# A fused window-mixer and routed-expert kernel: scatters in two groups and a normalisation in two halves

## The reference

```python
x = x + mixer(ln(x))                      # first half
t = x as tokens (16, 3136, 96)
t = t + experts(ln(t))                    # second half

def mixer(x):                             # windows of 7 x 7 positions
    w = ln(w, ln1_w, ln1_b)               # w: (1024 windows, 49 positions, 96)
    h[i] = w[i] @ Bm + h[i-1] @ A         # over the 49 positions
    xr = h @ Cm
    y = gelu(ln(xr, ln2_w, ln2_b) @ W1 + b1) @ W2 + b2    # 96 -> 384 -> 96
    return xr + y

def experts(t):                           # top 2 of 4 experts, exact gelu
    masked = softmax(t @ gate_w + gate_b) on the two best, renormalised
    return sum_e masked[e] * (gelu(t @ w1[e] + b1[e]) @ w2[e] + b2[e])
```

## Time and profile before

| | us |
|---|---|
| median of 3 runs | 1960.43 |
| lowest, highest | 1958.6, 1961.08 |
| the profiled execution | 1960.39 |
| its span | 1958.7 |
| PE busy in it | 1871.8 (96%) |
| ACT busy | 1599.1 (82%) |
| DVE busy | 1490.5 (76%) |
| POOL busy | 1355.4 (69%) |

### The profile page before, as it was taken

How to read it: one execution, slowest core, us unless ns; L and a number is a source line. 1 busy time by engine, 2 the same in 40 slices (tenths; PEclk the granted TensorE clock), 3 DMA queues, 4 the chain that set the end, 5 groups by cost and what they waited for, 6 DMA issues and landing times.

```text
span 1958.7 us, 36640 instructions
## 1 busy us (share of the span) xinstructions
PE 1871.8 (96%) x8883; PEld 1302.6 (67%) x8883; DVE 1490.5 (76%) x6676; ACT 1599.1 (82%) x3068; POOL 1355.4 (69%) x1097
## 2 busy tenths in 40 slices
PE   5979999999999999997599999999999999999996
PEld 3546666666666666664377777777777777777774
DVE  5767887788777877786477777777777777777775
ACT  3868887888888888875499989999999899999995
POOL 3357767776767677667477777777777777777775
PEclk9989999999999999998699999999999999999998
DMA  4042212222222222111666666666666666666662
GB/s 127 28 114 68 71 67 69 68 71 67 71 67 71 67 70 69 61 51 52 214 211 211 208 207 204 206 206 209 213 208 209 206 202 206 214 210 212 209 208 75
DMA packets 121158, 272.93 MB, mean 139 GB/s; under 512 B 26148, under 2 KB 34749, under 8 KB 120946
## 3 DMA queue, kind: packets, MB, share of 16 engines
q1 hardware_dynamic: 85840, 209.93, 35.6%
q0 software_dynamic: 32000, 58.87, 8.7%
q10 hardware_dynamic: 3106, 1.78, 0.3%
HBM read 204.47 MB, written 66.98 MB: 139 GB/s over the span
## 4 chain that ended last, share of the span: by engine, by line
PE 50%; POOL 27%; issue 20%; DVE 1%; DMA 1%; POOLq 0%; ACTq 0%; ACT 0%; SPq 0%; DVEq 0%
POOL sorted_rows L447 19%; PE mix_ps L1170 7%; PE mix_ps L1171 7%; PE mix_ps L1172 7%; POOL rstd_xt L436 7%; PE turn_ps L1156 4%; PE up_ps L1156 4%; PE turn_ps L1157 4%; PE turn_ps L1158 4%; PE up_ps L1157 4%; PE up_ps L1158 4%; PE tok_ps L1179 3%; PE y_ps L1142 2%; POOL rows L444 1%; POOL rstd_r L423 0%
## 5 line engine op out<-in xcount | busy, mean ns | idle before, releaser
L480 POOL DMA_INDIRECT out<-out_sb,idx x412 | 424.1, 1029 | 262.7 <-DVE out_sb L968 156.2
L924 DVE TENSOR_TENSOR g_lo<-g,g_hi 128x512 fp32r<-128x512 f32 x618 | 423.9, 686 | 198.5 <-ACT g_hi L613 198.5
L447 POOL DMA_INDIRECT sorted_rows<-rows,pos x392 | 383.3, 978 | 118.9 <-issue 104.8
L613 ACT CAST g_hi<-g 128x512 fp32r<-128x512 f32 x618 | 380.8, 616 | 13.1
L1048 PE MATMUL y_ps<-g,d_mlp 128*100 128x512 f32 x588 | 307.2, 604 | 6.5 <-ACT g L548 1.8
L469 POOL TENSOR_TENSOR ex<-euler,rows 128x16 f32<-128x16 f32 x103 | 305.2, 2963 | 10.1 <-DMA rows<-sorted_rows 9.7
L1170 PE MATMUL mix_ps<-g_hi,ew 128*96 128x512 f32 x618 | 244.1, 395 | 0.2 <-DVE g_lo L924 0.2
L1171 PE MATMUL mix_ps<-g_hi,ew 128*96 128x512 f32 x618 | 244.0, 395 | 0.0
L1172 PE MATMUL mix_ps<-g_lo,ew 128*96 128x512 f32 x618 | 243.7, 394 | 0.0
L548 ACT ACTIVATE g<-up_ps 128x512 f32<-128x512 f32 x294 | 172.7, 605 | 60.1 <-PE up_ps L1041 54.9
L423 POOL TENSOR_TENSOR rstd_r<-var_eps,neg_half 128x8 f32<-128x8 f32 x49 | 81.7, 1668 | 193.0 <-DVE var_eps L723 193.0
(11 more groups left out here) (181 smaller groups left out, 4164.9 us busy)
## 6 DMA issues: line engine op xcount, KB each, us to landing
ew<-expert_w SPq DMA_DIRECT2D x206, 384.0 KB, 4.2
ew<-expert_w SPq DMA_DIRECT2D x206, 288.5 KB, 3.5
rows<-sorted_rows SPq DMA_DIRECT2D x103, 394.0 KB
x_in<-in_x SPq DMA_DIRECT2D x49, 384.0 KB, 3.1
out<-out_sb,idx POOLq DMA_INDIRECT x412
sorted_rows<-rows,pos POOLq DMA_INDIRECT x392, 2.5
sorted_rows<-pad_rows SPq DMA_DIRECT2D x11, 394.0 KB, 5.0
expert_w<-w_hi SPq DMA_DIRECT2D x4, 192.0 KB, 3.9
```

The source lines that it names most:

```text
L447: pool.indirect_dma_start(out=sorted_rows[:, :], out_offset=bass.IndirectOffsetOnAxis(ap=pos[:, r, s:s + 1], axis=0), in_=rows[:, r, s, :] ...
L480: pool.indirect_dma_start(out=out_rows, out_offset=bass.IndirectOffsetOnAxis(ap=idx[:, r, s:s + 1], axis=0), in_=out_sb[:, r, s, :], in_of ...
L613: act.copy(g_hi[:, n % PART_RING, :], g[:, n % G_RING, :]).then_inc(hi_done, 1)
L924: dve.tensor_tensor(g_lo[:, n % PART_RING, :], g[:, n % G_RING, :], f(g_hi[:, n % PART_RING, :]), ALU.subtract).then_inc(lo_done, 1)
```

## The change

Three edits, all in phase 1.

- POOL: the eight scatters of a tile are issued as two groups of four. The first four (with the numbering) stay at the end of period t + 2. The last four stand at the start of period t + 3, ahead of `rstd_of_r`, behind a wait on `h_summed` for that period's input product. The loops get one more period for the last group.
- ACT: `normalise_xr` has two parts of four activations. Part 0 stands before Gelu 4 (it waits for the shift), part 1 behind Gelu 5 and the x_t copy. Part 0 signals a new semaphore `xr_half_ok`, part 1 `xr_n_ok`.
- PE: the xr transposes are issued as two groups of four, the first behind `xr_half_ok`, the second behind `xr_n_ok`. `turn_y(p,1)` moves from the end of period p to the next period, between `from_state` and `from_input`. The x transposes are issued by two calls without a wait between them.

```diff
--- before.py
+++ after.py
@@ -84,7 +84,7 @@
 
 
 def periods():
-    return range(-3, TILES + 2)
+    return range(-3, TILES + 3)
 
 
 class Region:
@@ -248,6 +248,7 @@
         dev_ok = sem("dev_ok")
         shift_x_ok, shift_r_ok, shift_t_ok = sem("shift_x_ok"), sem("shift_r_ok"), sem("shift_t_ok")
         xr_n_ok, in_gate_ok, x_xr_ok = sem("xr_n_ok"), sem("in_gate_ok"), sem("x_xr_ok")
+        xr_half_ok = sem("xr_half_ok")
         y_lo_ok, x2_ok = sem("y_lo_ok"), sem("x2_ok")
         gate_step, pos_step = sem("gate_step"), sem("pos_step")
         base_set, score_counted = sem("base_set"), sem("score_counted")
@@ -449,12 +450,17 @@
                         in_=rows[:, r, s, :], in_offset=None).then_inc(scattered[r], 16)
 
             for p in periods():
+                if tile(p - 3):
+                    if tile(p + 1):
+
+                        pool.wait_ge(h_summed, p + 2)
+                    scatter(p - 3, range(HALF_SUBS, SUBS))
                 if tile(p + 1):
                     rstd_of_r(p + 1)
                 if tile(p + 3) or tile(p - 1):
                     rstd_of_x_and_t(p + 3)
                 if tile(p - 2):
-                    scatter(p - 2, range(SUBS))
+                    scatter(p - 2, range(HALF_SUBS))
                 if p == -3:
                     pool.wait_ge(rstd_xt_ok, 1)
                     pool.memset(f(w_hi[C:P, :]), 0.0).then_inc(zeroed, 1)
@@ -524,14 +530,15 @@
                 if part == 1:
                     ins.then_inc(x_n_ok, 1)
 
-            def normalise_xr(t):
-                act.wait_ge(shift_r_ok, t + 1)
-                if t >= 1:
-                    act.wait_ge(xr_turned, t)
-                for s in range(SUBS):
+            def normalise_xr(t, part):
+                if part == 0:
+                    act.wait_ge(shift_r_ok, t + 1)
+                    if t >= 1:
+                        act.wait_ge(xr_turned, t)
+                for s in range(part * HALF_SUBS, (part + 1) * HALF_SUBS):
                     ins = act.activation(xr_n[:, s, :], mix_tok[:, s // HALF_SUBS, s % HALF_SUBS, 0:C], ACT.Identity,
                                          scale=rstd_r[:, t % 2, s:s + 1], bias=shift_r[:, s:s + 1])
-                ins.then_inc(xr_n_ok, 1)
+                ins.then_inc(xr_n_ok if part == 1 else xr_half_ok, 1)
 
             def normalise_rows(t):
                 act.wait_ge(shift_t_ok, t + 1)
@@ -581,16 +588,18 @@
                     gelu(p, 2)
                     gelu(p, 3)
                     copy_y(p, 0)
+                if tile(r):
+                    normalise_xr(r, 0)
+                if tile(p):
                     gelu(p, 4)
-                if tile(r):
-                    normalise_xr(r)
-                if tile(p):
                     gelu(p, 5)
                 if tile(p + 2):
                     act.wait_ge(x_turned, p + 3)
                     if p + 2 >= 1:
                         act.wait_ge(h_summed, p + 2)
                     act.copy(x_t[0:C, :], turn_ps[0:C, :]).then_inc(x_t_ok, 1)
+                if tile(r):
+                    normalise_xr(r, 1)
                 if tile(p):
                     copy_y(p, 1)
                 if p == -2:
@@ -1021,8 +1030,8 @@
                 pe.matmul(mix_ps[0:CG, BANK + (1 + KB) * EXPERTS:BANK + (1 + KB) * EXPERTS + 1], b_aug[0:C, :], b2_col[0:C, 0:1],
                           start=True, stop=True).then_inc(gate_sums, 1)
 
-            def to_channels(src):
-                for s in range(SUBS):
+            def to_channels(src, h):
+                for s in range(HALF_SUBS * h, HALF_SUBS * (h + 1)):
                     ins = pe.transpose(turn_ps[0:C, sub(s)], src[:, s, :], ident[:, :])
                 return ins
 
@@ -1084,6 +1093,9 @@
                 r = p + 1
                 if tile(r):
                     from_state(r)
+                if tile(p - 1):
+                    turn_y(p - 1, 1)
+                if tile(r):
                     from_input(r)
                 if tile(p):
                     up(p, 0)
@@ -1109,7 +1121,8 @@
                 if tile(p + 2):
                     turn.take(pe, x_t_ok, p + 3)
                     pe.wait_ge(x_n_ok, p + 3)
-                    to_channels(x_n[:, (p + 2) % 2, :, :]).then_inc(x_turned, 1)
+                    to_channels(x_n[:, (p + 2) % 2, :, :], 0)
+                    to_channels(x_n[:, (p + 2) % 2, :, :], 1).then_inc(x_turned, 1)
                 if p == -2:
                     gate_products()
                 if tile(p):
@@ -1118,10 +1131,10 @@
                     down(p, 5)
                 if tile(r):
                     turn.take(pe, y_lo_ok, r + 1)
+                    pe.wait_ge(xr_half_ok, r + 1)
+                    to_channels(xr_n, 0)
                     pe.wait_ge(xr_n_ok, r + 1)
-                    to_channels(xr_n).then_inc(xr_turned, 1)
-                if tile(p):
-                    turn_y(p, 1)
+                    to_channels(xr_n, 1).then_inc(xr_turned, 1)
 
             pe.wait_ge(table_step, 11)
             turn.take(pe, table_ok, 2)
```

## The result

| | before | changed |
|---|---|---|
| median (runs) | 1960.28 us (4) | 1939.15 us (4) |
| lowest, highest | 1958.6, 1961.08 | 1938.53, 1939.66 |
| profiled execution | 1960.39 us | 1939.66 us |
| its span | 1958.7 us | 1937.9 us |
| state copies of phase 1, 43 periods of | 17.764 us | 17.320 us |

The changed kernel is 1.1% faster: ratio 0.9893, 95% interval 0.9876 to 0.991. The forecast was 1942.7 us. Lines after about 450 carry new numbers; each row's operation names it.

The account below looks back on a forecast made before the run. PE's waiting, 0.54 us of each 17.76 us period, was taken as the bound, not POOL. 43 periods x 0.40 us plus 0.5 at the end made 17.7 us: 1960.4 to 1942.7 us, range 1935 to 1953.

Parts of the forecast that it names:

- `turn_y` behind the state products: On PE: moving turn_y(p,1) there removes the 0.19 us wait ahead of it; DVE's add, its reader, loses nothing.
- Rival (b): Only the moved turn_y pays, as xr's second half sits behind two copies and DVE's later shift pushes ACT: 1952 us, chance 0.13.
- The new stall of xr's second half: On PE: x_n transposes, x_t copy, then four activations on ACT make the second half 0.13 us late each period.
- The split's own price: One added semaphore on ACT and one already passed wait on PE: 0 to 0.05 us.
- DVE follows: DVE sets y_lo at 1.61 us after the state products start (S), statistics at 7.79, xr's shift at 11.87.
- The wait ahead of rstd_r: POOL's 2.72 us wait for the variance shrinks to 0.84 us, hiding the second scatter group's new wait at no cost.
- The one ahead of the fifth scatter: POOL's new wait for the input products, expected to last 0.5 to 1 us.
- (c): POOL sets the period, as the chain of waits says: 17.76 us stays, 1960 us, chance 0.06.
- (d): POOL's second scatter group ends late, delaying rstd_r, shift, xr halves and Gelus; slower from 1.4 us lateness, 1977 or 2012 us; chance 0.09.
- three signs of being wrong: Starts inside PE's block of ups and downs change, POOL's wait for the variance is gone, or the scatters lengthen.
- The ends: Phase 1's head gains nothing, the load gap swallowing it; the last tile gains 0.5 us; phase 2 is untouched.
- rival (a): No new stall, the x_t copy or xr's second half being a little earlier: period 17.22 us, 1936.7 us, chance 0.15.

Follow-up runs that it names:

- 5 + 3 split: The changed kernel with xr in parts of five and three activations instead of four and four, on ACT and PE: 1931.51 us, period 17.23 us.
- plain scatters: The changed kernel with a tile's eight scatters in one run again and no wait on the input products: 1937.84 us, period 17.32 us.
- 3 + 5 split: The changed kernel with xr in parts of three and five activations instead of four and four, on ACT and PE: 1954.65 us, period 17.74 us.

## Why the prediction was right, and where its sizes were off

1. **PE's own waiting is the bound, POOL is not.** Shown: the two edits that only take waiting off PE give the gain, the grouping on POOL gives none (taken out of the changed kernel, put alone into the kernel before, or held for the state copy), and the period fell to PE's own 17.23 us when the last wait went. Reading alone would have said the opposite, and the changed kernel's chain of waits still names the scatters first, with 20%. The occupancy of PE misled too: 17.66 of 17.76 before left 0.10 us, 0.44 were won, and with 17.32 of 17.32 busy the 5 + 3 split won another 0.09. That is what the Trainium skill's rule (Perfetto Trace Analysis, Identifying the Most-Contended Engine) warns of, and here the trace agrees.

2. **`turn_y` behind the state products.** Predicted 0.19, alone it measured 0.17. Its reader on DVE was not late. Rival (b), that only this edit pays, is out: the halves alone gave 0.22, and ACT still waits 0.18 us ahead of the x_t copy.

3. **The new stall of xr's second half.** Right in kind and place, mis-sized: 0.13 predicted, 0.09 measured. The terms of the chain came out as 1.07, 0.91 and 1.39 (predicted 1.08, 0.91, 1.40). The last one, the lag from ACT to PE, was priced at 0.12 and is where most of the difference lies. It was read from the end of the x_t copy (514.13) to PE's first product (514.25). The weight load ahead of that product started earlier:

```profile
514.17 0.12 PEld L1026 LDWEIGHTS turn_ps<-ident,xr_n 128*96 128x96 f32 x1 [0.61 <-ACT x_t L593]
```

So the 0.12 was 0.05 from ACT to the load (514.124 to 514.175 in the records' ns) and 0.08 from the load to the first product. In the changed kernel the load again starts 0.05 behind ACT's end (521.44 to 521.49), but the product starts with it, and the next one comes 0.04 later than usual: 0.09 in effect. With it the period is 17.32, not 17.36, and 43 periods give 19.1 us, not 17.2. The split's own price, put at 0 to 0.05, does not show: with 5 + 3, which has the same added semaphore and wait, the period is 17.23, against 17.22 worked out for a PE that never waits.

4. **DVE follows.** Predicted y_lo at S + 1.61, the statistics at 7.79, the shift at 11.87; measured 1.56, 7.62 and 11.70. Most of the 0.17 at the statistics is a wait that the 6.18 us between y_lo and them had held: in the trace before, DVE stood about 0.1 us for PE there. The wait of y_lo behind y_hi was 0.35, within the 0.3 to 0.4 named.

5. **POOL.** The wait ahead of rstd_r was predicted at 0.84 and measured at 1.02: the sum had counted the first scatter's 0.3 us of issue twice, and DVE's variance came 0.17 earlier than worked out. The one ahead of the fifth scatter was 1.4, not 0.5 to 1, since the first group ended at S + 2.85 (506.54 + 0.96) rather than 3.3. The rivals on POOL are settled: (c) is out, and the mechanism of (d) is real, it made a slower kernel when the group was held 2 us longer, but the change stays 1.3 us short of it. The four scatters beside DVE's statistics kept 0.96 us, so the lock-out that the Trainium skill describes (SBUF — State Buffer, Who interferes with whom) is not shown by these instructions. The prediction named three signs of being wrong. PE's block of ups and downs kept its starts (the x_n transposes start at S + 13.42, as worked out) and POOL's wait stayed, but the third came true in part: a scatter lengthened. It is the second of a tile, in the first group, beside DVE's gate work. Its end lies 0.80 us behind the start of DVE's `rank` reduction (0.81 at most) in all 33 cases, whatever its own start:

```profile
504.17 0.28 DVE L803 TENSOR_REDUCE rank<-beaten 128x32 f32<-128x128 f32 x1
```

504.17 + 0.80 = 504.97 = 503.83 + 1.14. A fixed end behind DVE's work, whatever the start, points to DVE holding the scatter; which of its instructions does so, and how, is not shown. It did no harm, since at most 0.3 us is lost where POOL had 1.0 in hand.

6. **The ends.** Predicted 0.5 us for the tail. The last copy stands 0.35 us later in its period, so the 0.95 above is 0.6 from S. POOL's wait for the last tile, against the earlier trace rows:

```profile
904.50 1.67 POOL L437 TENSOR_TENSOR rstd_xt<-var_eps,neg_half 128x8 f32<-128x8 f32 x1 [0.34 <-DVE var_eps L732]
```

It fell from 1.25 to 0.34. The instruction starts 32.15 us behind the last state copy instead of 33.10, which is the whole 0.95. The head was predicted at nothing, and 0.9 us came from there (1.3 from S). The same code differs by as much from run to run. The wait that ends the load gap is seen on DVE, first in the changed kernel, then in the same kernel run again:

```profile
109.51 1.38 DVE L721 BATCH_NORM_STATS2 stats<-x_in 128x6 f32<-128x96 f32 x8 [10.81 <-DMA x_in<-in_x]
```

```profile
106.99 1.38 DVE L721 BATCH_NORM_STATS2 stats<-x_in 128x6 f32<-128x96 f32 x8 [8.88 <-DMA x_in<-in_x]
```

This input comes 2.5 us earlier in the second execution of the same code, so the 0.9 us at the head are no effect that can be put down to the change. Over the groups of runs the gain of the changed kernel against its neighbours is 1957.1 - 1937.8 = 19.3 and 1957.3 - 1937.8 = 19.4 (plain scatters), where 43 x 0.444 and 0.6 for the tail make 19.7, with nothing from the head.

So 1942.7 was 3.5 us too high: 1.9 from the stall's size, about 1.3 from the head, 0.1 from the tail, less 0.1 in phase 2; the last 0.3 is the spread of the medians. By the time alone rival (a), 1936.7, was nearer than the forecast, but over a third of the miss is the head, which is luck. The period tells them apart: 17.32 against 17.36 in the forecast and 17.22 in (a), and there is a new stall.

## What to carry to other kernels

When a loop runs at one exact period, measure each group on the busiest engine from start to start and compare equal groups: the one that takes longer than its twin is where the period can shrink, and occupancy near 100% says nothing against it. Then follow the release of that group back; after an edit look for the next latest operand. Here its chain could be added up from rows to 0.05 us, well enough to choose a split (5 + 3 over 4 + 4) before running it. A wait added on an engine that already waits is free up to its idle time plus what its readers have in hand; here both could be read in the trace.

## What the runs showed of the hardware that was not expected

- The input loads behind the expert weights end 2.5 us apart between two executions of the same code (109.51 and 106.99), and the medians of the kernel before differ by 4 us between groups of runs (1960.3 to 1956.2), while the period of phase 1 is 17.32 us in both traces of the changed kernel. For changes in such a loop the period is the sharper measure.
- From the end of an ACT instruction to the weight load on PE that waits for it, it is 0.05 us behind a copy of 1024 columns (514.124 to 514.175, kernel before) and behind activations of 96 (521.438 to 521.489 in the changed kernel, 510.442 to 510.494 in the 3 + 5 split). What follows differs: the first product came 0.08 behind the load in the first case and with it in the second, where the next product then came after 0.15 us instead of 0.11. In the changed kernel the same signal of PE starts the copy on ACT at 508.63 and the scatter on POOL at 508.88, 0.25 later.
- A scatter issued by POOL seems to be held at times beside small DVE instructions (inferred from its end; no run changed DVE's work). Whenever the second scatter of a tile began between 0.46 and 0.20 us before DVE's `rank` reduction and was lengthened, it ended 0.80 to 0.81 us behind the reduction's start: 33 of 43 tiles in the changed kernel, and 36 of 43 with plain scatters. In the kernel before and with the groups alone it began 0.5 us or more before the reduction and took 0.96.
